# One of four quantization slots of an attention loop is issued behind the second score product instead of ahead of the first exponential

## The chip, the cores and the metric

The kernel runs on all 8 cores of one Trainium2 chip. Each core computes half of the rows of one batch element; the cores don't talk to each other. The metric is the device time of the slowest core in microseconds (us), lower is better. The engines of a core are named PE (TensorE, matrix products and transposes), DVE (VectorE), ACT (ScalarE), POOL (GpSimd) and SP (SyncE, which only issues DMAs here). Each engine takes its instructions strictly in the order in which the program lists them for it.

## The reference

One layer of a transformer with modulation ("adaln"), for x of 4 x 4096 x 1024:

```python
mod = (silu(c) @ wmod).reshape(4, 6, 1, 1024)     # sa, ca, ga, sb, cb, gb; ga, gb kept away from 0
h = layernorm(x) * (1 + ca) + sa
k, q, v = h @ Wk.T, h @ Wq.T, h @ Wv.T
e = q @ (k @ Wa.T).T                              # no scale
x = x + ga * (softmax(e) @ (v @ Wb.T))
h = layernorm(x) * (1 + cb) + sb
h = gelu(lora_linear(h, fake_quant(W_fc)))        # 1024 -> 4096
x = x + gb * lora_linear(h, fake_quant(W_proj))   # 4096 -> 1024

def fake_quant(w):                                # 8 bits, one scale for the tensor
    scale = max(abs(w)) / 127
    return clip(round(w / scale), -128, 127) * scale
```

## The kernel before

The program is five lists of instructions, one for each engine, filled by `em(engine, instruction, waits, inc)` in the order of the Python code. A wait is for a count of a semaphore (t, v, s, g for PE, DVE, ACT, POOL, and one for each kind of DMA), so the order of the `em` calls is the order of the work on each engine.

The phases: the modulation vector; the projected keys `ak_fm` and values `u_tm` for all 4096 rows and the queries for 2048 own ones; the attention loop (`ph5`); the feed-forward stage (`ph6`). The attention loop has 16 turns, ic = 0 to 15, each for 128 queries. One turn does this:

- Scores A (L1113): 32 matmuls of 128x512 fill `pE` (128x2048 in PSUM) for the first 2048 keys. L1122 on DVE takes the negated row maximum, L1127 on ACT the exponential into `alphaA`, which also frees `pE`.
- `_emit_pv(ic - 1, part=0)`, for the turn before: two groups of eight transposes (L1082) of `alphaB` through the one PSUM tile `pT1`, each group followed by a copy on DVE (L1090) into `alphaT`; then 32 matmuls of PV part 0 (L1211) into `pO`. It waits for both copies.
- Scores B (L1139): 32 matmuls into the same `pE` for the other 2048 keys. They wait for the exponential of A. Then the maximum L1148 and the exponential L1158 into `alphaB`, the rescaling of `alphaA` (L1167) and the sums of the rows.
- `_emit_pv(ic - 1, part=1)`: 32 more matmuls (L1224) and the result with the residual (L1233, L1239), stored by POOL. Then the transposes and copies of `alphaA`, and the next turn.

Between these, the weights of the feed-forward stage are quantized. A `quant_slot(k)` works on several of the 64 weight tiles of 128x1024 at once, one stage for each: the two signs (L959, L962 on ACT), two sums (L973, L978 on DVE), the scaling to bf16 (L991 on ACT), which also waits for all stores issued so far; for tile k the load of tile k+1 (L929, SP, behind L973), the product (L933), two rounds of a cast to int32 on DVE (L940) and back on ACT (L943), and the rounding error on POOL (L949); for tile k-6 eight transposes on PE (L1018) into `pT0`, the copy out of it on DVE (L1024), and the store by POOL (L1035). There are 70 slots; the store is part of one from slot 6 on.

`pump1()` issues the next slot. There are four calls in a turn, called a, b, c and d here: a stands between the A scores and their maximum L1122, b between L1122 and the exponential L1127, c behind the sums of the rows, d behind PV part 1. That makes 64 slots; the last six come after the loop. The first store is in slot c of ic = 1.

Of the kernel before, what the change touches and what calls it, by code (L numbers as in the profile page):

```python
# [22 lines left out]
class MK:  # L23
# [10 lines left out]
    def em(self, eng, fn, waits=(), inc=None, inc_n=None):  # L34
        if inc is not None and inc not in self.cnt:
            self.cnt[inc] = 0
        for snm, _v in waits:
            if snm not in self.cnt:
                self.cnt[snm] = 0
        if inc is not None and inc_n is None:  # L40
            inc_n = 16 if inc.startswith("d") else 1
        tok = None
        if inc is not None:
            self.cnt[inc] += inc_n
            tok = self.cnt[inc]
        self.ops[eng].append((fn, tuple((s, v) for (s, v) in waits if v), inc, inc_n))
        return tok
# [991 lines left out]
    def ph5(self):  # L1039
# [59 lines left out]
        def pump1():  # L1099
            if qslot_next[0] < 70:  # L1100
                self.quant_slot(qslot_next[0])
                qslot_next[0] += 1

        for ic in range(NQT):
# [6 lines left out]
            for oc in range(NCH):  # L1111
# [10 lines left out]
            t_mA = em("vector", lambda e: e.tensor_reduce(  # L1122
                out=s.mcol[:, 0:1], in_=s.pE[:], axis=AX.X, op=OP.max, negate=True),
                waits=[("t", t_eA), ("s", st["expA"]), ("v", st["rescale"])], inc="v")
            pump1()
            lb = (ic % 2) * 4
            t_expA = em("scalar", lambda e, lb=lb: e.activation(  # L1127
                out=s.alphaA[:], in_=s.pE[:], func=AF.Exp, bias=s.mcol[:, 0:1],
# [8 lines left out]
            for oc in range(NCH):  # L1137
                for jb in range(4):
# [6 lines left out]
                        waits=[("s", t_expA)],  # L1145
                        inc="t" if (oc == NCH - 1 and jb == 3) else None)
            st["qs_mm"][p] = t_eB
            t_mB = em("vector", lambda e: e.tensor_reduce(  # L1148
                out=s.mcol[:, 2:3], in_=s.pE[:], axis=AX.X, op=OP.max, negate=True),
                waits=[("t", t_eB), ("s", st["expA"])], inc="v")  # L1150
# [477 lines left out]
```

How the kernel before makes its waits and increments, by code:

```python
        def run_section(engname, engobj):  # L1522
            for fn, waits, inc, inc_n in self.ops[engname]:
                for sname, v in waits:
                    if last_wait[engname].get(sname, 0) < v:
                        engobj.wait_ge(sem[sname], v)
                        last_wait[engname][sname] = v
                instr = fn(engobj)
                if inc is not None:
                    instr.then_inc(sem[inc], inc_n)
```

## Time and profile before

| | us |
|---|---|
| median of 3 runs | 2918.19 |
| lowest and highest | 2917.12, 2918.60 |
| profiled execution, its own time | 2908.66 |
| profiled execution, span of the slowest core (core 5) | 2907.1 |
| spans of the 8 cores | 2893.3 to 2907.1 |

The profile shows one execution on its slowest core. "L1122" is line 1122 of the kernel. Times in the trace are counted from the first instruction. A busy time is the union of the instructions of an engine; the idle time in square brackets is what an engine stood still before an instruction, with the one that released it. PEclk is the clock granted to PE: 1.00 is 2.4 GHz, 0.50 is 1.2 GHz. Matmuls overlap by their pipeline, so a row of 32 ends about 0.1 us after the next row has begun.

### The profile page before, as it was taken

To read this page: it belongs to the slowest core of one execution; us is meant where nothing else is said; L and a number is where in the kernel's file an instruction comes from. 1 tells how busy PE (TensorE), PEld (TensorE's weight loads), DVE (VectorE), ACT (ScalarE), POOL (GpSimd) and SP (SyncE) were. 2 spreads that over 40 slices of the span, in tenths; PEclk is the share of its full clock that TensorE was granted. 3 is DMA by queue.
4 is the path that set the end of the run, shared out by engine and by line. 5 is a ranking of instruction groups with operands and counts; after the bars stand their busy time and mean duration, and the time that the engine had idled before them with its cause. 6 is when DMAs were issued, how large, how long until landed. Compare 5 with 4: busy or idle time off the path is not lost.

```text
span 2907.1 us, 24604 instructions; the slowest of 8 cores (2893.3 to 2907.1 us)
## 1 busy us (share of the span) xinstructions
PE 1700.8 (59%) x7994; PEld 760.3 (26%) x7994; DVE 996.5 (34%) x1745; ACT 757.2 (26%) x1290; POOL 419.6 (14%) x557
## 2 busy tenths in 40 slices
PE   3530504266565556556566556656615959869598
PEld 1210202132222222223233223322302323323233
DVE  3433333344444543444444454455311020110201
ACT  2320001122222231334334433344304123041230
POOL 0002222222333110122211222122100000000000
PEclk9865756577777877777787787877757979979799
DMA  5414242322222220122211222122142213122130
GB/s 143 163 53 134 84 132 94 107 77 70 71 69 66 71 71 26 47 84 76 80 62 69 87 82 70 62 73 90 52 159 83 64 58 102 47 81 62 58 102 29
DMA packets 90838, 233.36 MB, mean 80 GB/s; under 512 B 23860, under 2 KB 23989, under 8 KB 90696
## 3 DMA queue, kind: packets, MB, share of 16 engines
q1 hardware_dynamic: 64440, 160.32, 18.1%
q0 software_dynamic: 26272, 71.47, 7.1%
q8 instruction: 65, 1.06, 0.2%
q14 instruction: 61, 0.50, 0.1%
HBM read 193.85 MB, written 37.88 MB: 80 GB/s over the span
## 4 chain that ended last, share of the span: by engine, by line
PE 39%; DVE 17%; DMA 16%; ACT 11%; issue 11%; POOL 4%; SPq 1%; DVEq 1%; ACTq 0%; POOLq 0%
PE pE L1417 8%; PE pO L1459 8%; PE pO L1211 5%; DMA amst<-wpj_in 5%; PE pE L1139 4%; DMA amst<-wfc_in 4%; ACT h_stage L742 3%; POOL qt L949 3%; PE pE L1113 2%; DMA wm<-wmod_in 2%; PE pE L755 2%; DVE qkf L973 2%; ACT qkf L943 2%; DVE amx L634 2%; ACT h L1381 2%
## 5 line engine op out<-in xcount | busy, mean ns | idle before, releaser
L949 POOL TENSOR_TENSOR qt<-qt,qkf 128x1024 f32<-128x1024 f32 x64 | 149.9, 2342 | 817.0 <-ACT qkf L943 817.0
L1417 PE MATMUL pE<-h,wfcst 128*128 128x512 bf16 x1024 | 246.5, 384 | 3.7 <-DVE lora L1397 3.7
L1459 PE MATMUL pO<-wpj_sb,hid 128*128 128x512 bf16 x1024 | 226.3, 379 | 15.8 <-DVE outb L1475 12.1
L634 DVE TENSOR_REDUCE amx<-amst 128x1 f32<-128x256 f32 x256 | 106.8, 417 | 175.5 <-DMA amst<-wpj_in 93.3
L1211 PE MATMUL pO<-u_tm,alphaT 128*128 128x512 bf16 x512 | 146.0, 456 | 15.1 <-DVE alphaT L1090 15.1
L755 PE MATMUL pE<-h_stage,wkaT 128*128 128x512 bf16 x512 | 129.7, 421 | 29.9 <-ACT h_stage L742 29.9
L1113 PE MATMUL pE<-ak_fm,q_stg 128*128 128x512 bf16 x512 | 139.1, 439 | 0.5 <-DMA q_stg<-q_sc 0.5
L733 PE MATMUL pT<-idb,xnb 128*128 128x128 bf16 x256 | 32.4, 306 | 177.3 <-DVE xnb L721 177.3
L631 POOL DMA_DIRECT2D amst<-wfc_in x128 | 69.2, 541 | 461.2 <-DVE amx L639 305.0
L1432 ACT ACTIVATE hid<-pE,bfc_col 128x512 bf16<-128x512 f32 x128 | 88.0, 687 | 176.3 <-PE pE L1425 176.3
L1459 PEld LDWEIGHTS pO<-wpj_sb,hid 128*128 128x128 bf16 x1024 | 97.7, 98 | 137.9 <-issue 24.5
L943 ACT ACTIVATE qkf<-qki 128x512 f32<-128x512 int32 x128 | 80.6, 630 | 182.4 <-DVE qki L940 182.3
L1148 DVE TENSOR_REDUCE mcol<-pE 128x1 f32<-128x2048 f32 x16 | 36.7, 2292 | 258.2 <-PE pE L1139 258.2
L1417 PEld LDWEIGHTS pE<-h,wfcst 128*128 128x128 bf16 x1024 | 90.3, 98 | 127.9 <-issue 38.7
L1139 PE MATMUL pE<-ak_fm,q_stg 128*128 128x512 bf16 x512 | 114.5, 382 | 13.2 <-ACT alphaA L1127 13.2
L773 PE MATMUL pO<-wvbT,h_stage 128*128 128x512 bf16 x512 | 115.4, 379 | 7.4 <-DVE u_tm L785 6.7
L1082 PE MATMUL pT<-idb,alphaA 128*128 128x128 bf16 x256 | 32.9, 308 | 147.6 <-DVE alphaT L1090 141.7
L1492 POOL DMA_DIRECT2D out<-outb x16 | 8.6, 535 | 759.1 <-DVE outb L1486 759.1
L1224 PE MATMUL pO<-u_tm,alphaT 128*128 128x512 bf16 x512 | 113.1, 379 | 0.0
L1158 ACT ACTIVATE alphaB<-pE,mcol 128x2048 bf16<-128x2048 f32 x16 | 31.5, 1967 | 303.9 <-DVE mcol L1151 303.9
L1450 DVE CAST lora1p<-pE 16x512 bf16<-16x512 f32 x4 | 2.7, 679 | 312.1 <-PE pE L1442 312.1
L1018 PE MATMUL pT<-idb,qbf 128*128 128x128 bf16 x512 | 45.8, 242 | 105.0 <-DVE qbf L1024 105.0
(187 smaller groups left out, 2635.4 us busy)
## 6 DMA issues: line engine op xcount, KB each, us to landing
wfcst<-wfcq_sc SPq DMA_DIRECT2D x128, 256.0 KB, 2.6
wm<-wmod_in SPq DMA_DIRECT2D x32, 768.0 KB, 4.4
x_st<-x_in SPq DMA_DIRECT2D x48, 512.0 KB, 4.2
amst<-wfc_in POOLq DMA_DIRECT2D x128, 128.0 KB, 2.6
amst<-wpj_in POOLq DMA_DIRECT2D x128, 128.0 KB, 2.7
wst<-wfc_in SPq DMA_DIRECT2D x32, 512.0 KB, 3.3
wst<-wpj_in SPq DMA_DIRECT2D x32, 512.0 KB, 4.1
wfcq_sc<-qbf POOLq DMA_DIRECT2D x32, 256.0 KB, 2.4
```

Of the source, the lines that this page charges most:

```text
L634: t_r = em("vector", lambda e, c0=c0, c1=c1, first=first, p=p: e.tensor_reduce(out=s.amx[:, (c0 if first else c1):(c0 if first else c1) + ...
L755: t_mm = em("tensor", lambda e, oc=oc, ic=ic, g=g, sl=sl: e.matmul(out=s.pE[:, sl * 512:(sl + 1) * 512], lhsT=s.wkaT[:, ic * 1024 + oc * 1 ...
L773: t_mm = em("tensor", lambda e, tt=tt, vc=vc, ic=ic, g=g: e.matmul(out=s.pO[:, vc * 512:(vc + 1) * 512], lhsT=s.h_stage[:, ic * 512 + tt * ...
L943: t_kf = em("scalar", lambda e, qkf=qkf, hh=hh: e.activation(out=qkf[:, hh * 512:(hh + 1) * 512], in_=s.qki[:], func=AF.Copy), waits=[("v" ...
L949: t_dd = em("gpsimd", lambda e, qt=qt, qkf=qkf: e.tensor_tensor(out=qt[:], in0=qt[:], in1=qkf[:], op=OP.subtract), waits=[("s", t_kf)], in ...
L1113: t_eA = em("tensor", lambda e, oc=oc, jb=jb, p=p: e.matmul(out=s.pE[:, jb * 512:(jb + 1) * 512], lhsT=s.q_stage[p][:, oc * 128:(oc + 1) * ...
L1139: t_eB = em("tensor", lambda e, oc=oc, jb=jb, p=p: e.matmul(out=s.pE[:, jb * 512:(jb + 1) * 512], lhsT=s.q_stage[p][:, oc * 128:(oc + 1) * ...
L1211: em("tensor", lambda e, jc=jc, vc=vc: e.matmul(out=s.pO[:, vc * 512:(vc + 1) * 512], lhsT=s.alphaT[:, jc * 128:(jc + 1) * 128], rhs=s.u_t ...
L1224: t_pv = em("tensor", lambda e, jc=jc, vc=vc: e.matmul(out=s.pO[:, vc * 512:(vc + 1) * 512], lhsT=s.alphaT[:, jc * 128:(jc + 1) * 128], rh ...
L1417: t_mm = em("tensor", lambda e, ic=ic, oc=oc, p=p, sl=sl: e.matmul(out=s.pE[:, sl * 512:(sl + 1) * 512], lhsT=wfcst[p][:, ic * 128:(ic + 1 ...
L1432: pE_free[sl] = em("scalar", lambda e, oc=oc, sl=sl: e.activation(out=hid[:, oc * 512:(oc + 1) * 512], in_=s.pE[:, sl * 512:(sl + 1) * 512 ...
L1459: t_mm = em("tensor", lambda e, tt=tt, vc=vc, hc=hc: e.matmul(out=s.pO[:, vc * 512:(vc + 1) * 512], lhsT=hid[:, hc * 512 + tt * 128:hc * 5 ...
```

## The change

The second of the four calls, b, is moved. It stood between the maximum of A and its exponential. Now it stands behind the B scores, ahead of their maximum L1148. On ACT the slot then comes behind the exponential L1127 instead of before it. On DVE it comes behind the two copies of `alphaB`'s transposes and still before L1148; on PE its eight transposes come behind the B scores instead of before the transposes of `alphaB`. On SP its load comes behind the load of `x_st0`. On POOL nothing stands between the old place and the new one.

```diff
             t_mA = em("vector", lambda e: e.tensor_reduce(
                 out=s.mcol[:, 0:1], in_=s.pE[:], axis=AX.X, op=OP.max, negate=True),
                 waits=[("t", t_eA), ("s", st["expA"]), ("v", st["rescale"])], inc="v")
-            pump1()
             lb = (ic % 2) * 4
             t_expA = em("scalar", lambda e, lb=lb: e.activation(
                 out=s.alphaA[:], in_=s.pE[:], func=AF.Exp, bias=s.mcol[:, 0:1],
...
             st["qs_mm"][p] = t_eB
+            pump1()
             t_mB = em("vector", lambda e: e.tensor_reduce(
                 out=s.mcol[:, 2:3], in_=s.pE[:], axis=AX.X, op=OP.max, negate=True),
                 waits=[("t", t_eB), ("s", st["expA"])], inc="v")
```

## Rows read from the trace of the kernel before

**Rows 1.** The page: busy times, the chain by engine, one costly group.

```profile
PE 1700.8 (59%) x7994; PEld 760.3 (26%) x7994; DVE 996.5 (34%) x1745; ACT 757.2 (26%) x1290; POOL 419.6 (14%) x557
...
PE 39%; DVE 17%; DMA 16%; ACT 11%; issue 11%; POOL 4%; SPq 1%; DVEq 1%; ACTq 0%; POOLq 0%
...
L949 POOL TENSOR_TENSOR qt<-qt,qkf 128x1024 f32<-128x1024 f32 x64 | 149.9, 2342 | 817.0 <-ACT qkf L943 817.0
```

**Rows 2.** Windows: the attention loop; busy us (instructions) by engine, PE clock, DMA.

```profile
1134.00:2110.00 976.00, 594.86 (x3034) 291.07 (x3034) 445.20 (x607) 361.78 (x400) 196.48 (x137) 0.77 0.21 71
```

**Rows 3.** Timeline, PE, ic = 7, first half: start, us, line, count [idle before].

```profile
1546.54 9.64 PE L1113 MATMUL pE<-ak_fm,q_stg 128*128 128x512 bf16 x32
1556.02 0.61 PE L1018 MATMUL pT<-idb,qbf 128*128 128x128 bf16 x8
1557.64 0.61 PE L1018 MATMUL pT<-idb,qbf 128*128 128x128 bf16 x8 [1.01 <-DVE qbf L1024]
1558.09 0.61 PE L1082 MATMUL pT<-idb,alphaB 128*128 128x128 bf16 x8
1566.00 1.01 PE L1082 MATMUL pT<-idb,alphaB 128*128 128x128 bf16 x8 [7.30 <-DVE alphaT L1090]
1567.96 9.16 PE L1211 MATMUL pO<-u_tm,alphaT 128*128 128x512 bf16 x32 [0.94 <-DVE alphaT L1090]
1576.95 7.07 PE L1139 MATMUL pE<-ak_fm,q_stg 128*128 128x512 bf16 x32
```

**Rows 4.** Timeline, DVE, ic = 7, the same stretch.

```profile
1556.81 0.69 DVE L1024 COPY qbf<-pT 128x1024 bf16<-128x1024 bf16 x1 [2.80 <-PE pT L1018]
1557.42 2.28 DVE L1122 TENSOR_REDUCE mcol<-pE 128x1 f32<-128x2048 f32 x1
1559.61 1.22 DVE L973 SCALAR_TENSOR_TENSOR qkf<-wst,qkf 128x1024 f32<-128x1024 f32 x1
...
1565.17 0.68 DVE L1090 COPY alphaT<-pT 128x1024 bf16<-128x1024 bf16 x1
```

**Rows 5.** Timeline, ACT, ic = 7, the same stretch.

```profile
1557.31 1.15 ACT L959 ACTIVATE wst<-qt,kcol 128x1024 f32<-128x1024 f32 x1 [2.58 <-POOL qt L949]
...
1565.29 1.95 ACT L1127 ACTIVATE alphaA<-pE,mcol 128x2048 bf16<-128x2048 f32 x1
```

**Rows 6.** Groups by line, PE, 1134 to 2085 us: count, busy, mean ns, idle before.

```profile
L1211 PE MATMUL pO<-u_tm,alphaT 128*128 128x512 bf16 x480 | 136.9, 456 | 14.2 <-DVE alphaT L1090 14.2
...
L1224 PE MATMUL pO<-u_tm,alphaT 128*128 128x512 bf16 x480 | 106.0, 379 | 0.0
...
L1082 PE MATMUL pT<-idb,alphaB 128*128 128x128 bf16 x240 | 24.3, 263 | 115.2 <-DVE alphaT L1090 115.2
```

**Rows 7.** Timeline, DVE, ic = 7, the second maximum.

```profile
1584.20 2.29 DVE L1148 TENSOR_REDUCE mcol<-pE 128x1 f32<-128x2048 f32 x1 [16.39 <-PE pE L1139]
```

**Rows 8.** Timeline, PE, ic = 7, second half.

```profile
1596.24 1.01 PE L1018 MATMUL pT<-idb,qbf 128*128 128x128 bf16 x8 [4.87 <-DVE qbf L1024]
```

**Rows 9.** Timeline, PE, ic = 1.

```profile
1205.79 1.01 PE L1082 MATMUL pT<-idb,alphaB 128*128 128x128 bf16 x8 [9.63 <-DVE alphaT L1090]
```

**Rows 10.** Timeline, PE, ic = 0.

```profile
1156.34 8.47 PE L1139 MATMUL pE<-ak_fm,q_stg 128*128 128x512 bf16 x32 [13.22 <-ACT alphaA L1127]
```

**Rows 11.** Timeline, ACT, ic = 0.

```profile
1145.84 1.15 ACT L959 ACTIVATE wst<-qt,kcol 128x1024 f32<-128x1024 f32 x1 [2.57 <-POOL qt L949]
...
1152.84 1.28 ACT L1127 ACT_TABLE_LOAD   x1
```

**Rows 12.** The stores L1035: us from issue to landing.

```profile
DMA to landing us min/median/max: 2.3/2.9/4.5
```

**Rows 13.** Timeline, ACT, ic = 7, second half, slot c.

```profile
1591.24 1.13 ACT L991 ACTIVATE qbf<-qkf,kcol 128x1024 bf16<-128x1024 f32 x1
```

**Rows 14.** Windows around the fall of PE's clock, ic = 7; the clock is behind POOL.

```profile
1551.70:1562.00 10.30, 5.99 (x45) 3.31 (x43) 6.41 (x7) 4.70 (x5) 2.89 (x2) 1.00 0.20 72
1562.00:1572.20 10.20, 5.26 (x19) 2.25 (x20) 3.56 (x7) 3.21 (x4) 2.84 (x2) 0.50 0.32 127
```

## The prediction

> **What bounds the kernel now.** I read the page's busy times and its chain first [rows 1]. No engine is full: TensorE (PE) is busy 59% of the span, and the chain that ended last changes engine all the time (PE 39%, DVE 17%, DMA 16%, ACT 11%). So the reader should look for a hand-over between engines, not for a full engine. Then I cut out the stage that holds all of the change, the attention loop from 1134 to 2110 us: PE is busy 595 of its 976 us [rows 2].
>
> Then I read one turn, ic = 7, engine by engine. On PE [rows 3] the A scores (L1113) end at 1546.54 + 9.64 = 1556.18. Three groups of eight transposes follow, and then PE sits idle for 7.30 us until the second group of alphaB transposes (L1082) at 1566.00. That idle time is ended by DVE's alphaT copy. On DVE [rows 4] that copy (L1090) starts at 1565.17. The row maximum (L1122) had let DVE go by 1559.61; from there to 1565.17 DVE walks through the slot of pump call b, from its L973 to its L1024. On ACT [rows 5] the exponential of A (L1127) starts at 1565.29, behind the slot, which began at 1557.31, though its maximum was ready at 1559.7. So PE, with a half of the PV product ready but for two copies, waits for quantization work that nobody needs yet. Over the 15 turns ic = 1 to 15 this idle time sums to 115.2 us [rows 6]. After it PE has dense work: PV part 0 (9.16), the B scores (L1139, 7.07) [rows 3], and in that stretch DVE does nothing: it has waited 16.39 us when its next maximum, L1148, starts at 1584.20 [rows 7]. This is the room into which the change moves the slot.
>
> In the second half of a turn the DVE/ACT chain from L1148 through two more slots sets the next start of A; PE idles there for 4.87 us behind PV part 1 alone [rows 8].
>
> **The change, part by part.** Let Q be the end of the A scores and E the end of the B scores. Nothing is removed or added; one slot of each turn is issued later on all five queues.
>
> *DVE before the alphaT copies.* With the slot gone the first copy follows the maximum directly. It was let go at 1559.61 and started at 1565.17: 5.56 us earlier for ic = 7, whose PE idle was 7.30. For ic = 2 to 15 the idle mean is (115.2 - 9.63) / 14 = 7.54 [rows 6, 9], 0.24 more than in ic = 7, so 5.80 us a turn. I take the same for ic = 1, whose 9.63 us has no transposes of a store in it. 15 x 5.80 = 87.0 us.
>
> *ACT before the exponential.* It now starts right after the maximum, about Q + 3.6, and ends at Q + 5.7. PV part 0 begins at 1567.96 - 5.56 = 1562.40, Q + 6.2, and lasts over 8 us, so the B scores never wait for the exponential when ic > 0. For ic = 0 there is no PV work, and PE waits 13.22 us for the exponential [rows 10]. ACT began the slot at 1145.84 and the exponential's table load at 1152.84 [rows 11]; with the slot behind, the exponential moves ahead by this stretch, 7.0 us. The slot then runs beside the B scores, 8.47 us long [rows 10], and stays hidden.
>
> *The slot in its new place.* ACT starts it at Q + 5.7; now it takes ACT from 1557.31 to 1565.29, 8.0 us [rows 5], and GpSimd's subtraction follows (2.34 on average, L949) [rows 1]. It is over near Q + 16.1. E lies at Q + 6.2 + 9.1 + 6.9 = Q + 22.2. So it is hidden with 6 us to spare. Without that cover it would cost the 87 us again. On SP the load of x_st0 goes out ahead of the slot's weight load, and that load, issued behind the slot's L973 near Q + 8, isn't read before slot c, after E. On GpSimd the slot's store comes out after E.
>
> *What comes late.* The slot's eight transposes now stand behind the B scores on PE, its copy L1024 stands ahead of L1148 on DVE, and L1148 waits for it. The same pattern exists already after A [rows 3, 4]: transposes at 1556.02, L1024 at 1556.81, maximum at 1557.42, that is Q + 1.24. After B the maximum starts at 1584.20, 0.18 us after E = 1576.95 + 7.07 = 1584.02 [rows 3, 7]. The difference, 1.06 us, delays everything after L1148, up to the next A. It applies where the moved slot has a store, ic = 2 to 15: 14 x 1.06 = 14.8 us lost. Behind it on PE the next slot's transposes wait for this L1024, as in the 1.01 us idle after A [rows 3], so PV part 1 starts some 1.7 us later after E; PE sits idle for 4.87 us behind it now [rows 8], so this costs nothing. Slot c's L991 (ACT) waits for the moved store to land. Stores land in 2.3 to 4.5 us [rows 12]; issued near E + 2 it is down by E + 6.5, and L991 comes at E + 8.3 (1591.24 - 1584.02 + 1.06) [rows 13]. Nothing again.
>
> *PE's clock.* In ic = 7 the granted clock was 1.00 until 1562.0 and 0.50 until 1572.2 [rows 14]: it fell to 1.2 GHz 5.8 us after the dense work ended and rose 4.2 us after PV part 0 began. For this PV part 0 takes a mean of 136.9 / 15 = 9.12 us where PV part 1, at 2.4 GHz, takes 106.0 / 15 = 7.07 [rows 6]. With the change PV part 0 begins at Q + 6.2, just behind the fall at Q + 5.8, and the transposes between are fewer than now. So I leave it at 9.12. The bounds: at best the clock never falls, 15 x (9.12 - 7.07) = 31 us more saved, and 15 x 0.40 = 6 us on the transposes (1.01 to 0.61) [rows 3]; at worst all of PV part 0 runs at half clock, 14.1 instead of 9.12, which loses 75 us.
>
> The Trainium skill, "TensorE: Matmul & The Clock Gate", section "HAM oscillation — how this bites in real kernels", says that idle gaps between bursts of matmuls drop the clock and each burst then starts cold. The trace agrees (0.50 after the 7.30 us gap). The change shortens the longest gap ahead of PV part 0 to about 3 us; if the page's advice is read so that this keeps the clock up, the time is that of the warm rival below.
>
> **Sum.** 87.0 + 7.0 - 14.8 = 79.2 us saved. The profiled execution took 2908.66 us (span 2907.1), so it would be 2829.5. The median of the runs, 2918.19, is 9.5 us above that one; the saving is the same in both, so 2839 us. The remaining six slots come after the loop as now, and the feed-forward stage is untouched.
>
> **Rivals.**
> *Warm PV.* The clock holds through the shorter gap: 37 us more, 2802. For it: the gap falls from 7.3 to about 3 us. Against it: the fall at Q + 5.8 came with more transposes in the gap than there will be. 14%.
>
> *Partly given back.* The same forecast, but the clock comes back later in PV part 0 or the hand-over before L1148 costs 2 us instead of 1.06 (transposes, copy and maximum with nothing overlapped: 0.61 + 0.69 + gaps) [rows 3, 4]: 13 to 25 us lost, 2852 to 2864. 13%.
>
> *Zero sum, slower.* The slot on ACT and DVE does not run under the PV product, but is still on the way when the B scores end: then L1148 and the exponential of B wait for what those of A no longer wait for. The 87.0 and the 7.0 us are given back in full, and the 14.8 us of hand-over stay: 2918.2 + 14.8 = 2933. It needs the slot to end more than 6 us later than I work out; from 79.2 / 15 = 5.3 us of that kind a turn on, the kernel is slower. What could do it is a wait inside the slot for something that itself comes late (its weight load, the other store). The rows show neither late in this half. 4%.
>
> *Clock lost.* All of PV part 0 at 1.2 GHz: 75 us given back, 2914, within the error of no gain. Against it: the mean of 9.12 over 15 turns lies nearer to 7.07 than to 14.1. 2%.
>
> *No effect.* The copy or PV part 0 in fact waits for something else, so the idle time only changes its name, 2918. The end of the idle time in the rows is a copy right behind the slot's own, so 1%.
>
> **How the numbers follow.** The forecast itself has 66%, with an own range of 2824 to 2850. For 8 in 10 I take in most of the warm rival and the cheaper part of the partly-given-back one: 2804 to 2858. A measurement of this kernel tells about 0.2% (6 us) from no change. Faster by more than that: forecast, warm, partly, and half of the clock case, 94%; within 0.2%, the rest of that case and no effect, 2%; slower 4%.
>
> **What the profile after would show.** First alphaT copy right behind L1122; PE idle before the second alphaB transposes near 3 us instead of 7.3; Q to E near 22.2 instead of 1584.02 - 1556.18 = 27.8 us; PV part 0 at 9.1; L1148 at E + 1.24; the loop some 79 us shorter than its 976. I am wrong if DVE is still in the slot at E, if PV part 0 is 7.1 or above 11 us, or if L1148 comes later than E + 2.

## The result and the profile after

| | before | after |
|---|---|---|
| median of all runs, us | 2917.65 (10 runs) | 2824.73 (9 runs) |
| profiled execution, own time | 2908.66 | 2829.08 |
| profiled execution, span of the slowest core | 2907.1 | 2827.5 |

The ratio of after to before is 0.9695, with a 95% interval of 0.9674 to 0.9716. Against the 2918.19 of the prediction that is 2829 us (2823 to 2835): 89 us faster, where 79 were forecast (2839). The ratios here and below leave out executions that fell into a slower state, in which cores have a lower granted clock (here the 2986.61 us of the kernel before).

Spans and mean PE clock of two cores of the changed kernel. The slowest core is core 2:

```profile
core 2: 2827.5 us, clock 0.789
...
core 5: 2814.3 us, clock 0.789
```

The page of the changed kernel, busy times and the chain by engine. PE's share of the span reads the same. The matmuls are the same too: of the 7994, 140 records are missing in this trace, so PE's busy time is put somewhat too low (answers to [rows 1]):

```profile
PE 1682.1 (59%) x7854; PEld 756.4 (27%) x7994; DVE 996.8 (35%) x1745; ACT 754.8 (27%) x1290; POOL 420.7 (15%) x557
...
PE 41%; DMA 18%; DVE 16%; issue 10%; ACT 10%; POOL 3%; SPq 1%; DVEq 1%; ACTq 0%; POOLq 0%
```

PE's timeline in turn ic = 7 of the changed kernel, core 2 (start, us, count; idle before in brackets), against [rows 3, 8]:

```profile
1501.33 9.12 PE L1113 MATMUL pE<-ak_fm,q_stg 128*128 128x512 bf16 x31
...
1510.73 0.61 PE L1082 MATMUL pT<-idb,alphaB 128*128 128x128 bf16 x8
1514.70 0.61 PE L1082 MATMUL pT<-idb,alphaB 128*128 128x128 bf16 x8 [3.36 <-DVE alphaT L1090]
1516.26 8.46 PE L1211 MATMUL pO<-u_tm,alphaT 128*128 128x512 bf16 x31 [0.94 <-DVE alphaT L1090]
1524.56 7.07 PE L1138 MATMUL pE<-ak_fm,q_stg 128*128 128x512 bf16 x31
1531.46 0.61 PE L1018 MATMUL pT<-idb,qbf 128*128 128x128 bf16 x8
1533.09 0.61 PE L1018 MATMUL pT<-idb,qbf 128*128 128x128 bf16 x8 [1.01 <-DVE qbf L1024]
...
1556.49 1.86 PE L1113 MATMUL pE<-ak_fm,q_stg 128*128 128x512 bf16 x4 [0.35 <-DMA q_stg<-q_sc]
```

Q is now 1501.33 + 9.12 = 1510.45 and E is 1524.56 + 7.07 = 1531.63. The idle time before the second group of alphaB transposes is 3.36 us instead of 7.30, these transposes take 0.61 instead of 1.01, and Q to E takes 21.18 instead of 27.84. The moved slot's transposes stand at 1531.46, behind the B scores; the next slot's wait 1.01 us behind them. Q to PV part 0 falls by more than the idle time does, because the moved slot's own group of transposes and its wait of 1.01 us are gone from ahead of the alphaB groups as well.

DVE in the same turn, against [rows 4, 7]:

```profile
1511.68 2.28 DVE L1122 TENSOR_REDUCE mcol<-pE 128x1 f32<-128x2048 f32 x1
1513.87 0.68 DVE L1090 COPY alphaT<-pT 128x1024 bf16<-128x1024 bf16 x1
...
1517.30 1.22 DVE L973 SCALAR_TENSOR_TENSOR qkf<-wst,qkf 128x1024 f32<-128x1024 f32 x1 [1.19 <-ACT wst L959]
...
1521.93 0.43 DVE L940 CAST qki<-qt 128x512 int32<-128x512 f32 x1 [0.88 <-ACT qkf L943]
1532.25 0.69 DVE L1024 COPY qbf<-pT 128x1024 bf16<-128x1024 bf16 x1 [9.89 <-PE pT L1018]
1532.86 2.28 DVE L1148 TENSOR_REDUCE mcol<-pE 128x1 f32<-128x2048 f32 x1
```

The first alphaT copy starts at 1513.87, as the maximum lets DVE go. The slot (1517.30 to the cast at 1521.93) lies under PE's dense work, then DVE waits 9.89 us for the transposes. L1148 starts at 1532.86, E + 1.23. ACT's exponential, and GpSimd's subtraction with which the slot's work ends, against [rows 5]:

```profile
1514.11 1.97 ACT L1126 ACTIVATE alphaA<-pE,mcol 128x2048 bf16<-128x2048 f32 x1 [4.59 <-DVE mcol L1122]
...
1523.23 2.34 POOL L949 TENSOR_TENSOR qt<-qt,qkf 128x1024 f32<-128x1024 f32 x1 [10.38 <-ACT qkf L943]
```

The exponential starts at Q + 3.7, the subtraction ends at Q + 15.1, and E is Q + 21.2: 6 us to spare, as forecast.

Groups by line on PE over the loop's turns (count, busy, mean ns, idle before), against [rows 6]:

```profile
L1113 PE MATMUL pE<-ak_fm,q_stg 128*128 128x512 bf16 x496 | 139.5, 447 | 9.0 <-ACT wst L959 4.7 <-DMA q_stg<-q_sc 3.1 <-issue 0.7
...
L1082 PE MATMUL pT<-idb,alphaB 128*128 128x128 bf16 x240 | 18.7, 222 | 49.8 <-DVE alphaT L1090 49.8
```

The 115.2 us of idle time before the alphaB transposes are 49.8 (51.6 on core 5). New is the idle time of 9.0 us before the A scores (L1113). In ic = 0 PE now waits 5.98 us for the exponential instead of 13.22 [rows 10]:

```profile
1143.75 8.69 PE L1138 MATMUL pE<-ak_fm,q_stg 128*128 128x512 bf16 x32 [5.98 <-ACT alphaA L1126]
```

Windows around the fall of PE's clock in ic = 7 (busy time by engine, then the granted clock), against [rows 14]:

```profile
1505.50:1515.70 10.20, 6.40 (x46) 3.48 (x45) 6.08 (x8) 3.27 (x4) 2.89 (x2) 1.00 0.35 129
1515.70:1519.10 3.40, 2.85 (x7) 1.04 (x8) 2.10 (x3) 3.31 (x5) 0.00 (x0) 0.50 0.00 0
1519.10:1530.00 10.90, 10.85 (x51) 4.95 (x51) 2.27 (x4) 1.64 (x3) 2.34 (x1) 1.00 0.16 50
```

The clock falls at 1515.7, Q + 5.3, where it fell at Q + 5.8 before. But it is low for 3.4 us only, and it is back 2.8 us after PV part 0 has begun.

### The profile page after: what moved, and what is told of

Same layout as the page of the kernel before. It is cut to its first block, busy times and chain, and to the rows that moved or that the text cites. A ratio compares the mean times of both kernels' runs of the same rounds, so it can differ in the third digit from the quotient of the medians.

```text
span 2827.5 us, 24464 instructions; the slowest of 8 cores (2804.2 to 2827.5 us)
## 1 busy us (share of the span) xinstructions
PE 1682.1 (59%) x7854; PEld 756.4 (27%) x7994; DVE 996.8 (35%) x1745; ACT 754.8 (27%) x1290; POOL 420.7 (15%) x557
## 4 chain that ended last, share of the span: by engine, by line
PE 41%; DMA 18%; DVE 16%; issue 10%; ACT 10%; POOL 3%; SPq 1%; DVEq 1%; ACTq 0%; POOLq 0%
PE pE L1417 8%; PE pO L1459 8%; DMA amst<-wfc_in 6%; PE pO L1211 5%; PE pE L1113 5%; PE pE L1138 4%; ACT h_stage L742 3%; DMA amst<-wpj_in 3%; DMA wm<-wmod_in 2%; PE pE L755 2%; DVE amx L634 2%; ACT h L1381 2%; POOL q_sc L812 2%; POOL qt L949 1%; PE pE L1425 1%
## 5 line engine op out<-in xcount | busy, mean ns | idle before, releaser
L1113 PE MATMUL pE<-ak_fm,q_stg 128*128 128x512 bf16 x496 | 139.5, 447 | 9.0 <-ACT wst L959 4.7
L1024 DVE COPY qbf<-pT 128x1024 bf16<-128x1024 bf16 x64 | 44.0, 688 | 203.9 <-PE pT L1018 185.5
L973 DVE SCALAR_TENSOR_TENSOR qkf<-wst,qkf 128x1024 f32<-128x1024 f32 x64 | 78.4, 1225 | 85.4 <-ACT wst L959 85.1
```

Of the source, the lines that this page charges most:

```text
L1113: t_eA = em("tensor", lambda e, oc=oc, jb=jb, p=p: e.matmul(out=s.pE[:, jb * 512:(jb + 1) * 512], lhsT=s.q_stage[p][:, oc * 128:(oc + 1) * ...
```

## The experiments

Q, E, the loop (first A score to last PV matmul) and the turn are as in the prediction. Means are over ic = 1 to 15 of one core. The diffs are against the changed kernel. First the same core, core 5, in both kernels:

| core 5, us | before | changed | times 15 | forecast |
|---|---|---|---|---|
| Q to PV part 0 | 12.01 | 5.73 | -94.2 | -87.0 |
| PV part 0 | 9.12 | 8.47 | -9.8 | 0 |
| E to the next A (x 14) | 23.36 | 24.36 | +14.0 | +14.8 |
| A scores | 8.69 | 9.06 | +5.6 | 0 |
| Q to B in ic = 0 (once) | 13.2 | 6.0 | -7.2 | -7.0 |
| loop | 975.4 | 885.6 | -89.8 | -79.2 |

The five parts add up to -91.6; behind the last turn's B scores the loop takes 1.8 us more. PE's clock explains two of the rows. A row of 32 matmuls takes 7.07 us at a clock of 1.00, and time at 0.50 costs half its length. On core 5 the clock was at 0.50 for 4.2 us of PV part 0 and 3.3 us of the A scores a turn before, and for 2.9 and 4.0 us after: halves of 2.1 and 1.6, then 1.4 and 2.0, which are what the rows take over 7.07.

A third value of the clock, 0.81, showed on some cores in most of the profiles below. Where it did, the text says so.

**1. The slot behind the exponential only.** Is it ACT's exponential or DVE's copies that PE waited for?

```diff
             st["expA"] = t_expA
+            pump1()
             if ic > 0:
                 self._emit_pv(ic - 1, st, emit_trans, part=0)
...
             st["qs_mm"][p] = t_eB
-            pump1()
```

> Slot b right behind the exponential of A, but still ahead of the alphaB transposes and their copies. Theory (PE waits for DVE's alphaT copies, which stand behind the slot): the first copy still waits for the whole slot, and the slot itself starts later, since ACT now does the exponential first (slot on ACT from Q + 5.7 instead of Q + 1.1). The copies come 2 to 3.5 us a turn later than in the kernel before, the 7 us of ic = 0 are saved: 2918 + 15 x (2 to 3.5) - 7 = 2941 to 2964, slower than before. Rival (what PE waits for is the exponential of A behind the slot on ACT): nearly the whole gain comes, about 2830.

Measured: 2958.5 us, ratio 1.0131 (1.0092 to 1.0170). ACT, DVE and then PE of this kernel in ic = 7, core 4:

```profile
1575.05 1.97 ACT L1126 ACTIVATE alphaA<-pE,mcol 128x2048 bf16<-128x2048 f32 x1 [5.09 <-DVE mcol L1122]
...
1577.01 1.14 ACT L959 ACTIVATE wst<-qt,kcol 128x1024 f32<-128x1024 f32 x1
```

```profile
1578.25 1.23 DVE L973 SCALAR_TENSOR_TENSOR qkf<-wst,qkf 128x1024 f32<-128x1024 f32 x1 [3.34 <-ACT wst L959]
...
1583.82 0.68 DVE L1090 COPY alphaT<-pT 128x1024 bf16<-128x1024 bf16 x1
```

```profile
1584.65 1.01 PE L1082 MATMUL pT<-idb,alphaB 128*128 128x128 bf16 x8 [10.74 <-DVE alphaT L1090]
```

The exponential starts right behind the maximum (1575.05), which gains nothing but the 7.2 us of ic = 0: the slot now begins with ACT's signs at 1577.01, its DVE part at 1578.25, and the first copy comes at 1583.82. PE's idle time is 10.74 us in this turn, and PV part 0 begins 3.1 us a turn later than in the kernel before (2 to 3.5 expected). On cores 0, 1, 4 and 5 the clock was at 0.81 for 85 us of the loop; on the other four the loop took 1013 us, 38 more than the 975 before, so the loss is not the clock's. The forecast mechanism holds, the rival falls: the copies on DVE were what PE waited for.

**2. The slot out of the way, but without cover.** It is issued next to slot c, behind the sums of the rows.

```diff
             st["qs_mm"][p] = t_eB
-            pump1()
...
             st["linv"] = t_linv
             pump1()
+            pump1()
```

> Slot b behind the sums of the rows together with slot c: it is out of the way of the alphaT copies and of the exponential of A, as in the changed kernel, but nothing covers it: two slots in a row, then PV part 1, slot d. Theory (the gain needs both: the slot away from ahead of the copies, and a place under PV part 0 and the B scores): E - Q stays at 21 us, L1148 is back at E + 0.2, and the second half gets one slot's chain more, about 8 to 9.5 us from one slot to the next: E to the next A 32 to 33 us, 2829 + 15 x (8 to 9.5 - 1.06) = 2933 to 2956, slower than before the change. Rival (any place behind the copies gives the gain, because the second half has slack too): 2830 or less.

Measured: ratio 1.0176 (1.0153 to 1.0199), 2968.4 us beside a kernel before of 2913.6 at best on this chip. Q to E is 22.1, where 21 was expected, and E to the next A 33.0 us (24.4 in the changed kernel), where 32 to 33 were. By the ratio the time is 2970 on the scale of the prediction, above the expected 2933 to 2956; the excess is the 1 us of Q to E (PV part 0 takes 9.3 us here) and an E to the next A at the upper end. PE of this kernel, core 6, ic = 7:

```profile
1602.49 7.07 PE L1138 MATMUL pE<-ak_fm,q_stg 128*128 128x512 bf16 x31
1609.40 0.61 PE L1018 MATMUL pT<-idb,qbf 128*128 128x128 bf16 x8
1622.14 1.01 PE L1018 MATMUL pT<-idb,qbf 128*128 128x128 bf16 x8 [12.13 <-DVE qbf L1024]
```

Behind the B scores PE waits 12.13 us for the second slot's transposes. The gain needs both halves: the slot away from ahead of the copies, and a place under PV part 0 and the B scores. Without the second half the change would be slower than no change.

**3. The hand-over ahead of L1148.** The slot is issued ahead of the B scores, so that its transposes and L1024 don't stand between E and L1148.

```diff
                 self._emit_pv(ic - 1, st, emit_trans, part=0)
+            pump1()
             t_eB = None
...
             st["qs_mm"][p] = t_eB
-            pump1()
```

> Slot b behind PV part 0 and ahead of the B scores: the same place as in the changed kernel on DVE, ACT and GpSimd, but its transposes stand ahead of the B scores on PE, so that L1024 is done long before L1148. Theory of the hand-over (1.06 us a turn from the transposes and L1024 ahead of L1148): L1148 back at E + 0.2, E to the next A 1.06 us shorter, PE longer by the transposes (0.45 us): 14 x 1.06 - 14 x 0.45 = 9 us faster than the changed kernel, near 2820. Rival (the hand-over is hidden or comes from something else): 6 us slower than the changed kernel, 2835.

Measured: 2831.3 us, ratio 0.9705 (0.9679 to 0.9732), so no different from the changed kernel. On core 1 L1148 is back at E + 0.11 and E to the next A at 23.34: the 1.0 us of hand-over is real. But Q to E grew from 21.1 to 21.7 and the A scores from 9.05 to 9.4, and the turn stayed at 54.4 us (54.5 in the changed kernel). Of the first, 0.4 is the transposes on PE. The rest, 0.2, and the second are the clock: it was at 0.50 for 3.2 us of PV part 0 and 4.7 us of the A scores a turn, where core 5 of the changed kernel had 2.9 and 4.0, though in all a turn has 20.3 us at 0.50 (20.4). Neither the 9 us of my theory nor the 6 us of loss came; what moves the kernel's time as a whole is also that cores 4 to 7 had 90 us of a granted clock of 0.81 (see 6), with loops of 901 to 904 us beside 883 to 886 on the others.

**4. The idle time before A.** The queries of the next turn are loaded one turn ahead.

```diff
-            t_q = em("sync", lambda e, ic=ic, p=p: e.dma_start(
-                out=s.q_stage[p][:], in_=s.q_hbm[ic]),
-                waits=[("t", st["qs_mm"][p])] + qbar, inc="d_q%d" % p)
-            st["qs"][p] = t_q
+            for icq in ((0, 1) if ic == 0 else (ic + 1,)):
+                if icq < NQT:
+                    pq = icq % 2
+                    st["qs"][pq] = em("sync", lambda e, ic=icq, p=pq: e.dma_start(
+                        out=s.q_stage[p][:], in_=s.q_hbm[ic]),
+                        waits=[("t", st["qs_mm"][pq])] + qbar, inc="d_q%d" % pq)
+            t_q = st["qs"][p]
```

> The changed kernel with the load of the next turn's queries issued one turn ahead (SP, ahead of the turn's weight loads). Theory: on cores 2 and 3 of the changed kernel E to the next A is 25.1 instead of 24.4 us because this load lands late; with it early all cores have 24.4, the loops of cores 2 and 3 fall from 900 by 10 us or more toward the 886 of the others, and the slowest core with them: 2815 to 2820. Rival (cores 2 and 3 are longer by PE's clock or by other DMAs): no change, 2829, and E to the next A stays at 25 on some cores.

Measured: 2826.4 us, ratio 0.9694 (0.9668 to 0.9721), the same as the changed kernel. Landing of the query load in the changed kernel, core 2 and then core 5:

```profile
DMA to landing us min/median/max: 2.6/5.3/7.7
```

```profile
DMA to landing us min/median/max: 2.5/4.3/5.3
```

On core 2 the load takes up to 7.7 us. It is issued some 6 us ahead of A (1550.43 for an A at 1556.49), so there it can come last; the profile puts 4.7 of the 9.0 us down to ACT's L959, but this experiment shows whose they are. With the early load, the same group on core 2 has 1.9 us of idle time:

```profile
L1116 PE MATMUL pE<-ak_fm,q_stg 128*128 128x512 bf16 x496 | 143.2, 456 | 1.9 <-issue 1.3
```

E to the next A is 24.4 to 24.5 us on all cores. So the stretch is explained; the time is not. The loops of cores 2 and 3 were still 899 and 896 us, because PE's clock was lower there in the first turns: at 0.81 for 92 and 89 us, which neither had in the changed kernel. Windows of core 2 (the clock is the first number behind POOL):

```profile
1195.70:1223.00 27.30, 23.53 (x106) 10.50 (x106) 9.94 (x16) 7.26 (x9) 3.45 (x2) 0.81 0.06 20
1311.80:1335.70 23.90, 19.43 (x100) 9.10 (x100) 8.48 (x14) 7.13 (x9) 2.89 (x2) 1.00 0.10 34
```

**5. Work in the gap.** 40 transposes of the identity behind the first group of alphaB transposes and 10 behind the second, into `pT0`, read by nobody. (The ten stand ahead of PV part 0, not ahead of the first group as the expectation has it.) Nothing is left out of the computation.

```diff
                 self.pTst["tr"][pp] = t_tr
+                for _ in range((40, 10)[grp] if half else 0):
+                    em("tensor", lambda e: e.transpose(
+                        out=s.pT0[:, 0:128], in_=s.idb[:, :], identity=s.idb[:, :]),
+                        waits=[self.pTst["free"][0]])
```

> The changed kernel with 40 extra transposes of the identity into pT0 (nobody reads them) ahead of the second group of alphaB transposes and 10 ahead of the first, so that PE has work in the gap between the A scores and PV part 0; nothing is left out of the computation. Theory (PV part 0 takes 8.95 us and not 7.07 because the gap lets the clock fall): granted clock 1.00 through the gap, PV part 0 at 7.1 us, 15 x 1.9 = 28 us faster than the changed kernel if the extra work fits into the gap of 3.4 us, near 2801; up to 1 us a turn of it is lost if it doesn't. Rival (PV part 0 is slow for another reason, its operands or the copies beside it): PV part 0 stays at 8.5 to 9 us, 2829 or later.

Measured: 2815.9 us, ratio 0.9655 (0.9623 to 0.9687). PE of core 0 in ic = 7, then PV part 0 over the loop, then a window from behind this gap with its clock:

```profile
1499.48 2.39 PE L1090 MATMUL pT<-idb 128*128 128x128 bf16 x40 [0.56 <-DVE qbf L1024]
1502.27 0.61 PE L1082 MATMUL pT<-idb,alphaB 128*128 128x128 bf16 x8 [0.40 <-DVE alphaT L1094]
1502.71 0.72 PE L1090 MATMUL pT<-idb 128*128 128x128 bf16 x10
```

```profile
L1215 PE MATMUL pO<-u_tm,alphaT 128*128 128x512 bf16 x512 | 113.1, 379 | 6.2 <-DVE alphaT L1094 6.2
```

```profile
1512.00:1520.80 8.80, 7.79 (x49) 3.97 (x48) 2.38 (x2) 0.00 (x0) 1.69 (x2) 1.00 0.01 4
```

With the gap filled the clock stays at 1.00, PV part 0 takes 7.07 us a turn (113.1 / 16), its begin is unchanged, and the loop is 859 us instead of 885.6 on this and three more cores. The term for PV part 0 is a clock term and nothing else. On cores 2 to 5, which had some 110 us of a granted clock of 0.81 (see 6), the loop was 877 to 881 us, and with these slowest cores only some 12 us of the expected 28 reach the kernel's time, by ratios whose intervals overlap.

**6. Both.** The gap filled and the queries early.

> The changed kernel with both edits: the extra transposes in the gap and the early load of the queries. In the run with the gap filled, four cores had a loop of 860 us and four of 877 to 881, with 24.8 instead of 24.4 us from E to the next A and an E - Q of 20.25 instead of 19.7. Theory (the late load of the queries is what the slower four lose from E to the next A): that stretch is 24.4 on all cores, 14 x 0.4 = 6 us from the slowest core: near 2810. Rival (the slower four lose by disturbed first turns, the load is hidden anyway): 2816 as without the early load.

Measured: 2821.6 us, ratio 0.9659 (0.9612 to 0.9706): the rival. E to the next A was 24.4 us on all cores, as the theory said, but cores 2, 3, 6 and 7 had loops of 894 to 908 us beside 860 on the others. Core 6, two stretches between falls of the clock, and the B scores in the first:

```profile
1399.20:1443.60 44.40, 38.51 (x221) 19.66 (x223) 20.80 (x29) 14.93 (x18) 7.71 (x5) 0.81 0.19 60
1515.30:1552.80 37.50, 30.52 (x203) 16.34 (x205) 18.53 (x27) 14.40 (x17) 5.79 (x4) 1.00 0.20 69
```

```profile
1419.62 8.58 PE L1145 MATMUL pE<-ak_fm,q_stg 128*128 128x512 bf16 x31
```

The granted clock there is 0.81, neither 0.50 nor 1.00, and the 32 matmuls of the B scores take 8.58 us instead of 7.07.

**7. Room for a second slot.** Slot c is issued together with b, ahead of the B scores; the queries are early.

```diff
                 self._emit_pv(ic - 1, st, emit_trans, part=0)
+            pump1()
+            pump1()
             t_eB = None
...
             st["qs_mm"][p] = t_eB
-            pump1()
...
             st["linv"] = t_linv
-            pump1()
```

> Slots b and c both behind PV part 0 and ahead of the B scores, none behind the sums of the rows; slot d and a stay; queries loaded early. Theory (in the second half of a turn the DVE/ACT chain of the slots c and d sets the next A, and under PV part 0 and the B scores DVE has 10 us free): E to the next A falls from 24.4 to about 17 us (slot d starts right behind the exponential of B, without waiting for slot c's subtraction on GpSimd), while E - Q grows from 21.1 to about 23.2 by the two groups of transposes on PE and the wait between them. 15 x (7.4 - 2.1) = 80 us faster than the changed kernel, near 2750. Rival (DVE and ACT have no room for a second slot there: it is still on the way at E and L1148 inherits it): E to the next A 22 or more, 2825 or slower.

Measured: 2773.8 us, ratio 0.9449 (0.9404 to 0.9493), 2757 against the 2918. PE and then DVE of core 1, from PV part 1 in one turn to the B scores in the next:

```profile
1493.98 7.07 PE L1227 MATMUL pO<-u_tm,alphaT 128*128 128x512 bf16 x32
...
1510.04 8.95 PE L1116 MATMUL pE<-ak_fm,q_stg 128*128 128x512 bf16 x32
...
1524.79 8.38 PE L1214 MATMUL pO<-u_tm,alphaT 128*128 128x512 bf16 x32 [0.94 <-DVE alphaT L1090]
1533.00 0.61 PE L1018 MATMUL pT<-idb,qbf 128*128 128x128 bf16 x8
1534.62 0.61 PE L1018 MATMUL pT<-idb,qbf 128*128 128x128 bf16 x8 [1.01 <-DVE qbf L1024]
1535.07 7.07 PE L1143 MATMUL pE<-ak_fm,q_stg 128*128 128x512 bf16 x32
```

```profile
1502.84 1.22 DVE L973 SCALAR_TENSOR_TENSOR qkf<-wst,qkf 128x1024 f32<-128x1024 f32 x1
...
1507.80 0.68 DVE L1024 COPY qbf<-pT 128x1024 bf16<-128x1024 bf16 x1
```

Q to E is 23.6 to 23.7 us and E to the next A 16.1, loops of 797 us instead of 886 (-89, expected -80). Slot d's part on DVE now begins at 1502.84, behind the result of PV part 1, and its last copy starts at 1507.80; there is no slot c in front of it. The rival (no room) falls.

**8. Slot c behind the B scores instead.** As in 7, but with the second `pump1()` behind `st["qs_mm"][p] = t_eB`.

> As the run with both slots moved, but slot c behind the B scores on PE (slot b stays ahead of them), so L1024 of slot c is ahead of L1148. Theory of the hand-over: E - Q is 1.5 us shorter than there (one group of transposes and no wait between the two), but L1148 starts at E + 1.3 or later; both cancel, 2745 to 2760. Rival (the hand-over costs nothing): 2730.

Measured: 2751.2 us, ratio 0.9398 (0.9354 to 0.9442); the interval overlaps that of 7. Cores 0 and 1 had 330 us of a granted clock of 0.81 and cores 4 to 7 had 94 to 99. On cores 2 and 3, which had none, Q to E is 22.6 to 22.7 us (23.7 in 7), L1148 starts at E + 1.5 (E + 0.3), and E to the next A takes 16.7 (16.1). So a half of the 1.1 us comes back; with A scores of 8.6 to 8.8 us (9.0) the turn takes 48.0 instead of 48.7 us and the loop 785 instead of 797. The two don't quite cancel, but no more than that is at stake.

**9. Both slots moved, gap filled.**

> Both slots ahead of the B scores, queries early, and the 40 and 10 extra transposes in the gap ahead of PV part 0. Theory (clock): PV part 0 at 7.1 us as in the run with the filled gap. But here the second group of slot transposes must wait for DVE in any case: slot c is over near Q + 22 on DVE, so with the B scores ending earlier (E at Q + 21.7) L1148 waits for the slot instead. So at most 1 us a turn of the 1.5 is kept: 10 to 15 us faster than without the extra transposes. Rival (PE still sets E): 25 us faster.

Measured: 2743.3 us, ratio 0.9341 (0.9275 to 0.9407), the lowest value here, but it rests on two of six executions and its interval overlaps that of 8. PE of core 1:

```profile
1495.88 8.11 PE L1120 MATMUL pE<-ak_fm,q_stg 128*128 128x512 bf16 x32
...
1509.79 7.07 PE L1218 MATMUL pO<-u_tm,alphaT 128*128 128x512 bf16 x32 [0.39 <-DVE alphaT L1094]
1516.70 0.61 PE L1018 MATMUL pT<-idb,qbf 128*128 128x128 bf16 x8
...
1518.76 7.07 PE L1147 MATMUL pE<-ak_fm,q_stg 128*128 128x512 bf16 x32
```

PV part 0 is 7.07 us, Q to E 21.66, L1148 at E + 0.37, and the loop 762 to 765 us on six cores instead of 797: 33 us, more than my 10 to 15. That is the rival's reading, PE still sets E, and its 25 was too little as well: PV part 0 gives 1.9 us a turn and not 1.5. (Cores 4 and 5 had 122 us of a granted clock of 0.81 and loops of 781 and 778.) The step that failed was that slot c would hold up L1148. Slot c on DVE begins behind slot b's L1024, whose transposes stand behind PV part 0 (at Q + 12.7 here, 1516.70, and Q + 14.0 in 7, 1533.00). So when PV part 0 gets shorter, slot c moves ahead too. It just fits: in the turn shown E is 1525.83, and L1148 starts at 1526.02, right behind slot c's copy.

## Why the prediction was right, point by point

- *What PE waited for.* Right: the copies behind the slot. Experiment 1 took the slot from ahead of the exponential alone and lost 1.3%; PE's idle time before the second group fell from 115.2 to 51.6 us in the loop of core 5 when the copies came first.
- *DVE before the copies, 87.0 us.* On core 5 the begin of PV part 0 came 6.28 us a turn earlier, 94.2 us. Of the difference of 7.2 us, 6 are the transposes at 0.61 instead of 1.01 us, which I had counted only as a bound, since they now run at Q + 4.3, before the clock falls at Q + 5.3.
- *ic = 0, 7.0 us.* 7.2 measured.
- *The cover.* Right: the slot ends under the B scores with the 6 us to spare that were forecast (9.89 on DVE), and experiment 2 shows the price without it, E to the next A of 33.0 us and a slower kernel. That is the mechanism of the zero-sum rival; it didn't come about in the changed kernel.
- *What comes late, 14.8 us.* 14.0 on core 5, L1148 at E + 1.23 as worked out from the pattern after A. Experiment 3 removes it, but the turn doesn't get shorter, so it is a real delay and no gain to be had alone.
- *PE's clock.* This term was mis-sized: I left PV part 0 at 9.12 us and it took 8.47, 9.8 us less over the loop. The fall came about where I put it, and the warm rival with it fell: with a longest gap of 3.36 us the clock still went to 0.50 ahead of PV part 0. What I had wrong is that the low stretch would reach as far into PV part 0 as before; it went from 10.2 to 3.4 us in ic = 7, and its part behind the begin of PV part 0 from 4.2 to 2.8. Experiment 5 shows the rest of this term at its bound, 7.07 us. Against it the A scores took 0.37 us more a turn, 5.6 us, which I had not counted; that is the clock too, 4.0 us at 0.50 in them instead of 3.3.
- *Not foreseen.* On the two slowest cores, 2 and 3, the loop was 900 us, 15 more than on core 5: E to the next A of 25.0 to 25.1, of which the late query load is shown by experiment 4, and PV part 0 of 8.95, in the later turns up to 10.0. Behind most turns with the late load the next turn's PV part 0 was longer too; that the one shifts the other against the clock's falls is argued, not shown. So the slowest core of each profile gives 975.4 - 900.3 = 75 us, where core 5 alone gives 89.8.

The sum is 10 us short of the measured 89 and of core 5's 89.8, because the two terms that I had kept as bounds, transposes and clock, came in by a part. The two profiled executions are 2908.66 - 2829.08 = 79.6 us apart, which looks like the forecast 79.2 to the microsecond. That is luck: the loss on cores 2 and 3, which I had not foreseen, took back what the two terms had brought.

## What to carry to other kernels

Where two chains share an in-order queue, look for the copy or the wait that the busiest engine needs and see which filler work stands directly ahead of it; then put the filler where that engine has dense work, not merely behind the copy. Both are needed, and the rows tell beforehand: how long the filler is, and how long its engine already waits in the new place. When such a move has worked, see which second piece of filler fits into the same room before polishing hand-overs of a microsecond: slot c was worth another 2.5 to 3%, the place of a hand-over nothing in experiment 3 and at most 0.7 us a turn in experiment 8.

## What the runs showed of the hardware

- Besides 1.00 and 0.50 the granted clock had a third value, 0.81, in the loop. It came on 2 to 6 cores and always on both of a pair of neighbours: in experiment 1 on cores 0, 1, 4 and 5 (85 us), in 3 on cores 4 to 7 (some 90), in 4 on 2 and 3 (some 90), in 5 on 2 to 5 (some 110), in 6 on 2, 3, 6 and 7 (338 us of the loop on core 2, 474 on core 6), in 8 on 0 and 1 (330) and 4 to 7 (some 95), in 9 on 4 and 5 (122). It was absent in the loops of the profiles of the kernel before, the changed one and experiments 2 and 7. 32 matmuls of 512 columns took 8.58 us there instead of 7.07. What sets it off stays open: within one execution some cores had it and others, with the same program, did not.
- The Trainium skill, "TensorE: Matmul & The Clock Gate", section "Seeing it yourself", tells of a peak-current limit that takes a whole die to 13/16 of the clock once three of its cores run dense matmuls. The value agrees (0.81); the traces show it on all four cores of a die (experiments 3 and 8), but also on two cores with the other two of their die at 1.00 (experiments 1, 4, 5, 6 and 9).
- In experiment 3 the turns of cores 0 to 3 take 54.4 to 54.6 us like the 54.5 of the changed kernel's core 5, though L1148 comes 1.1 us earlier and the A scores take anything from 8.3 to 9.4 us. What a microsecond on the path is worth isn't read from the path alone when PE's clock falls twice a turn.
- The profile's releaser can be wrong by name: 2.31 us before an A score were put down to ACT's L959 and went away with the earlier DMA.
